# A token-mixing vision tower in one kernel: the last doubling of two tables cut in two, GpSimd's shift table started during the powers, new load orders

## What is computed

```python
# layer 1: a diagonal state-space kernel, 256 positions long, for each channel h
dA = (1 + dtA / 2) / (1 - dtA / 2)              # complex, (256, 64)
V = exp(log(dA)[:, :, None] * arange(256))      # powers 0 .. 255 of dA
h = 2.0 * einsum('chn,hnl->chl', C * B, V).real # (16, 256, 256)
# layer 2: attention without softmax (16 heads, elu + 1), MLP 256 -> 1024 -> 256, on layernorm(h)
h = h + attn_block(layernorm(h))
# layer 3: a soft decision tree of depth 8 (255 gates, 256 leaves), on layernorm(h)
h = h + tree_ffn(layernorm(h))
```

## Time and profile before

| what | before |
|---|---|
| median of 3 runs | 499.4 us (498.92 to 500.75) |
| profiled execution, its own time | 499.2 us |
| its span | 497.4 us |
| PE busy | 441.4 us, 89% |
| DVE busy | 347.8 us, 70% |
| ACT busy | 296.0 us, 60% |
| POOL busy | 191.1 us, 38% |
| DMA | 30.95 MB, 39903 packets |

### The profile page before, as it was taken

The page is one execution under the profiler, slowest core; times in us unless marked ns, Lnnn a source line. Parts: engine busy times, 40 slices in busy tenths (PEclk is TensorE's granted clock), DMA queues, the critical chain, the costliest instruction groups (busy, mean ns, idle before and its releaser), DMA issues.

```text
span 497.4 us, 11488 instructions
## 1 busy us (share of the span) xinstructions
PE 441.4 (89%) x3881; PEld 402.0 (81%) x3881; DVE 347.8 (70%) x814; ACT 296.0 (60%) x617; POOL 191.1 (38%) x188
## 2 busy tenths in 40 slices
PE   0375778999999999999999999999999999998985
PEld 0165667887798898989989988988988988988984
DVE  4899987987876786546486486476476476485775
ACT  4734655879867686358438348348347357356542
POOL 0299996742423011417207207207206306306120
PEclk9867999999999999999999999999999999999996
DMA  4532678436353102001002002002002001001002
GB/s 128 180 137 76 169 187 228 99 97 169 95 138 98 43 22 63 2 2 43 0 2 84 0 0 84 0 0 84 0 0 84 0 0 42 0 0 45 0 2 84
DMA packets 39903, 30.95 MB, mean 62 GB/s; under 512 B 19520, under 2 KB 35264, under 8 KB 39872
## 3 DMA queue, kind: packets, MB, share of 16 engines
q1 hardware_dynamic: 28944, 27.48, 18.6%
q10 hardware_dynamic: 10928, 3.08, 2.7%
HBM read 17.97 MB, written 12.58 MB: 61 GB/s over the span
## 4 chain that ended last, share of the span: by engine, by line
PE 69%; DVE 11%; issue 5%; POOL 5%; ACT 5%; DMA 3%; SPq 1%; POOLq 0%; DVEq 0%; ACTq 0%
PE PS L336 19%; PE PS L338 18%; PE PS L337 18%; PE PS L1655 5%; PE PS L1780 3%; PE PS L1697 3%; PE PS L1628 2%; POOL Wb L514 2%; DVE XY L1052 2%; DVE lTl L1348 1%; POOL Wa L514 1%; DMA aim<-in_a_im 1%; DMA craw<-in_c_ri 1%; PE PS L1664 1%; DVE PS L1052 1%
## 5 line engine op out<-in xcount | busy, mean ns | idle before, releaser
L1377 DVE TENSOR_TENSOR gl<-PS,gh 128x512 fp32r<-128x512 f32 x56 | 38.7, 690 | 62.3 <-ACT gh L867 31.9
L864 ACT ACTIVATE PS<-PS,fc1bias 128x512 f32<-128x512 f32 x56 | 36.7, 655 | 75.3 <-PE PS L338 74.4
L336 PE MATMUL PS<-fc2h,gh 128*128 128x256 f32 x256 | 73.6, 288 | 2.9 <-DVE gl L1377 1.5
L567 POOL TENSOR_SCALAR pst<-mv 128x4 f32<-128x4 f32 x15 | 4.2, 283 | 185.1 <-DVE pst L1361 185.1
L338 PE MATMUL PS<-fc2l,gh 128*128 128x256 f32 x256 | 71.5, 279 | 0.0
L337 PE MATMUL PS<-fc2h,gl 128*128 128x256 f32 x256 | 71.4, 279 | 0.0
L336 PE MATMUL PS<-x2Th,fc1h 128*128 (+2 forms) x144 | 54.5, 379 | 0.0
L336 PEld LDWEIGHTS PS<-fc2h,gh 128*128 128x128 f32 x256 | 48.0, 188 | 7.0 <-DVE pst L1361 1.6
L337 PE MATMUL PS<-x2Th,fc1l 128*128 (+2 forms) x144 | 53.0, 368 | 0.0
L338 PE MATMUL PS<-x2Tl,fc1h 128*128 (+2 forms) x144 | 52.9, 367 | 0.0
L337 PEld LDWEIGHTS PS<-fc2h,gl 128*128 128x128 f32 x256 | 48.2, 188 | 1.0
(11 more groups left out here) (256 smaller groups left out, 1408.9 us busy)
## 6 DMA issues: line engine op xcount, KB each, us to landing
h<-h_scratch SPq DMA_DIRECT2D x16, 256.0 KB, 3.4
q_scratch<-qe SPq DMA_DIRECT2D x16, 256.0 KB, 2.3
qf<-q_scratch SPq DMA_DIRECT2D x16, 256.0 KB, 2.9
out_tokens<-outb SPq DMA_DIRECT2D x14, 256.0 KB, 2.3
h_scratch<-tokev ACTq DMA_DIRECT2D x10, 256.0 KB, 3.1
craw<-in_c_ri SPq DMA_DIRECT2D x16, 128.0 KB, 2.5
craw<-in_c_ri SPq DMA_DIRECT2D x32, 64.0 KB, 2.4
h_scratch<-tokev SPq DMA_DIRECT2D x6, 256.0 KB, 2.9
```

What stands on the lines that cost most here:

```text
L336: pe.matmul(dst, ah, bh, start=start, stop=False, **kw)
L864: act.activation(bank(j % 2), bank(j % 2), ACT.Gelu, bias=fc1bias[:, j:j + 1]).then_inc(gact, 1)
L1377: dve.tensor_tensor(gl[:, j % 2, :], bank(j % 2), gh[:, j % 2, :].bitcast(F32), ALU.subtract).then_inc(gldone, 1)
```

## The change

It has five parts, and the diff below is cut to their core.

1. **X and Y.** The third doubling (m = 4) is done for channels 0 to 127 before chunk 0, and for channels 128 to 255 (chunks 8 to 15) behind the sum of chunk 7. ACT copies the powers for the second half into bank 6 in chunk 0, and waits for the second half before it puts out the tables of chunk 8. The first doubling uses bank 0 for its products, the third bank 2.
2. **The shift table.** POOL starts after the sixth instruction of the powers instead of after the last, forms the third power into a row of its own, reads the first three powers from the compact table, and no longer waits for ACT's copies. ACT makes eight copies into Er and Ei later, behind the copy for the third doubling. DVE waits for them before chunk 0.
3. **PSUM.** The imaginary parts of the powers 8, 16 and 32 and of U are kept in PSUM.
4. **Loads.** One half of the imaginary input goes over SP in front of the others, and two of the four loads of B over ACT; the qkv weights go behind B. Later, chunk 11's coefficients and chunk 12's go between the first loads of images, one after each of the first two.
5. **Orders behind chunk 9.** On ACT the tables of chunk 12 move ahead of the result of chunk 10, and the operands of chunk 12 behind the first `y_high`; on DVE statistics and low parts are interleaved with the products of chunks 11 and 12. PE does the second half of the bias matmuls only when the first product of chunk 0 is done.

```diff
@@ power(): where the powers lie
+        def u_imag(d):
+            return (PS[:, 2, H:2 * H], PS[:, 3, 0:H], PS[:, 3, H:2 * H])[d]
...
+                return [pwb[:, j - 3, 0, :], (PS[:, 6, H:2 * H], PS[:, 7, H:2 * H], PS[:, 2, 0:H])[j - 3]]
+            return [U[:, 0, j - 6, :], u_imag(j - 6)]
@@ sync
-            sp.dma_start(qkvraw[:, :, :], qkvT.rearrange("(k p) o -> p k o", p=P)).then_inc(ld_qkv, 16)
+            sp.dma_start(aim[halves[1], :], a_im).then_inc(ld_aim, 16)
             for r, rows in enumerate(halves):
                 sp.dma_start(btab[rows, 0, :], b_ri[r]).then_inc(ld_b, 16)
-                sp.dma_start(btab[rows, 1, :], b_ri[1 - r]).then_inc(ld_b, 16)
+            sp.dma_start(qkvraw[:, :, :], qkvT.rearrange("(k p) o -> p k o", p=P)).then_inc(ld_qkv, 16)
...
-            for n in range(2, FIRST):
+            for n in range(2, FIRST - 1):
                 load_c(n // 2, n % 2)
             for par in range(2):
                 sp.wait_ge(h0st[par], CREDIT + 16 * (PAIRS // 2))
-            for s in range(4):
+            for s in range(2):
                 load_h0(s)
-            load_c(FIRST // 2, FIRST % 2)
+                load_c((FIRST - 1 + s) // 2, (FIRST - 1 + s) % 2)
+            for s in range(2, 4):
+                load_h0(s)
@@ gpsimd
-            pool.wait_ge(dve_set, DVE_POWERS)
-            rotated(Er[:, :, 2], Ei[:, :, 2], pw[:, 0, 0, :], pw[:, 0, 1, :], pw[:, 1, 0, :], pw[:, 1, 1, :],
+            pool.wait_ge(dve_set, DVE_Z + 6)
+            rotated(pw[:, 2, 0, :], pw[:, 2, 1, :], pw[:, 0, 0, :], pw[:, 0, 1, :], pw[:, 1, 0, :], pw[:, 1, 1, :],
                     tE[:, :, 0])
-            pool.wait_ge(e_out, 6)
@@ scalar
+            act.dma_start(aim[0:N, :], a_im).then_inc(ld_aim, 16)
             for r in range(2):
-                act.dma_start(aim[r * N:(r + 1) * N, :], a_im).then_inc(ld_aim, 16)
+                act.dma_start(btab[r * N:(r + 1) * N, 1, :], b_ri[1 - r]).then_inc(ld_b, 16)
...
+            act.wait_ge(pool_set, 1 + 6)
+            for e in range(4):
+                for x, t in enumerate((Er, Ei)):
+                    w = pw4[:, x, :] if e == 3 else pw[:, e, x, :]
+                    act.activation(t[:, :, e], w, ACT.Copy).then_inc(e_out, 1)
             act.wait_ge(pe_set, 1)
...
             act.wait_ge(gated, 1)
+            act.activation(PS[:, 6, H:2 * H].rearrange("p (x h) -> p x h", x=2), pwb[:, 2, :, P:H],
+                           ACT.Copy).then_inc(pw_out, 1)
             opened(0, 1)
...
             closed(3, 0)
             paired_operands(4, 0)
+            closed(3, 1)
+            act.wait_ge(dve_set, DVE_XY)
+            for par in range(2):
+                paired_tables(4, par)
             m_unshifted(4, 0)
...
+            tables(SINGLE + 2)
             token_row(SINGLE)
-            tables(SINGLE + 2)
+            y_high(0)
             operands(SINGLE + 2)
-            y_high(0)
@@ vector
+            dve.wait_ge(pw_out, 3)
+            doubled(slice(0, P), 4, *(w[:, 0:P] for w in halves_of(1)), bank(2))
...
+            dve.wait_ge(e_out, 8)
...
-            for n in range(6, SINGLE - 1):
-                overlapped(n, n % 2)
+            overlapped(6, 0)
+            product_sums(7, 1)
+            dve.wait_ge(pw_out, 4)
+            doubled(slice(P, H), 4, PS[:, 6, H:H + P], PS[:, 6, H + P:2 * H], bank(2))
+            assert count[0] == DVE_XY, count[0]
+            dve.wait_ge(pool_set, POOL_TABLES + 6)
+            first_product(8, 0)
+            second_product(8, 0)
+            overlapped(8, 0)
             product_sums(SINGLE - 1, 1)
...
             unsummed_products(SINGLE)
+            norm1_stats(0)
             single_product(SINGLE + 1, 0)
             single_product(SINGLE + 1, 1)
-            norm1_stats(0)
+            norm1_apply(0)
             single_sums(SINGLE + 1)
-            norm1_apply(0)
+            single_product(FIRST, 0)
             norm1_stats(1)
+            y_low(0)
+            single_product(FIRST, 1)
             norm1_stats(2)
-            y_low(0)
             for n in range(FIRST, CHUNKS):
                 s = n - FIRST
-                single_product(n, 0)
-                single_product(n, 1)
+                if s > 0:
+                    single_product(n, 0)
+                    single_product(n, 1)
+                single_sums(n)
                 if s == 0:
                     norm1_apply(1)
                     norm1_apply(2)
-                single_sums(n)
@@ tensor, the bias matmuls
             for j in range(JH):
+                if j == JH // 2:
+                    pe.wait_ge(prodX, CREDIT + 1)
```

More of the change, by code:

```diff
@@ L52 @@
 DVE_U = DVE_POWERS + 4 + 4 + 4 + 5
-DVE_W1 = DVE_U + 3
+DVE_XY = DVE_U + 5
+DVE_W1 = DVE_XY + 3
 DVE_W2 = DVE_W1 + 2 + KD
@@ L178, in vit_tower @@
         pw = sb("pw", [P, 3, 2, H])
+        pw4 = sb("pw4", [P, 2, H])
         phase1_end = max(phase1_end, cursor[0])
@@ L318, in sums_before @@
             return max([x for x in range(c) if sums_bank(x) == sums_bank(c)], default=-1)
+        def u_imag(d):
+            return (PS[:, 2, H:2 * H], PS[:, 3, 0:H], PS[:, 3, H:2 * H])[d]
         def power(j):
-            if j < 3:
+            if j < 2:
                 return [pw[:, j, x, :] for x in range(2)]
+            if j == 2:
+                return [pw4[:, x, :] for x in range(2)]
             if j < 6:
-                return [pwb[:, j - 3, x, :] for x in range(2)]
-            return [U[:, 0, j - 6, :], ui[:, j - 6, :]]
+                return [pwb[:, j - 3, 0, :], (PS[:, 6, H:2 * H], PS[:, 7, H:2 * H], PS[:, 2, 0:H])[j - 3]]
+            return [U[:, 0, j - 6, :], u_imag(j - 6)]
         def apart(eng):
@@ L648, in _ @@
             act.activation(Y[:, :, 0], btab[:, 1, :], ACT.Copy, scale=-2.0).then_inc(b_out, 1)
+            act.wait_ge(ld_qkv, 16)
+            act.activation(qkvh[:, :, :], qkvraw[:, :, :], ACT.Copy).then_inc(act_set, 1)
             act.wait_ge(ld_const, 16 * 6)
             act.activation(minus[:, :], ident, ACT.Copy, scale=-1.0).then_inc(minus_set, 1)
-            act.wait_ge(ld_qkv, 16)
-            act.activation(qkvh[:, :, :], qkvraw[:, :, :], ACT.Copy).then_inc(act_set, 1)
             act.wait_ge(dve_set, DVE_Z)
@@ L666, in _ @@
             act.wait_ge(dve_set, DVE_POWERS)
-            for j in range(2):
-                act.activation(bank((6, 7)[j]), pwb[:, j, :, :].rearrange("p x h -> p (x h)"),
-                               ACT.Copy).then_inc(pw_out, 1)
-            for e, j in ((0, 0), (1, 1), (3, 2)):
-                for x, t in enumerate((Er, Ei)):
-                    act.activation(t[:, :, e], pw[:, j, x, :], ACT.Copy).then_inc(e_out, 1)
+            act.activation(PS[:, 6, 0:H], pwb[:, 0, 0, :], ACT.Copy).then_inc(pw_out, 1)
+            act.wait_ge(dve_set, DVE_POWERS + 4)
             for d in range(ND - 1):
-                if d == 2:
-                    act.wait_ge(dve_set, DVE_POWERS + 4)
-                act.activation(U[:, 1, d, :], ui[:, d, :], ACT.Copy, scale=sgn[:, 0:1]).then_inc(u_out, 1)
+                act.activation(U[:, 1, d, :], u_imag(d), ACT.Copy, scale=sgn[:, 0:1]).then_inc(u_out, 1)
+            act.activation(pwb[:, 2, 1, :], PS[:, 2, 0:H], ACT.Copy).then_inc(u_out, 1)
+            act.activation(PS[:, 7, 0:H], pwb[:, 1, 0, :], ACT.Copy).then_inc(pw_out, 1)
             for c in range(3):
@@ L797, in _ @@
             paired_tables(1, 0)
-            with act.Fori(0, 3) as it:
+            with act.Fori(0, 2) as it:
                 for par in range(2):
                     next_opened(it, par)
-            paired_tables(4, 1)
+            next_opened(2, 0)
+            paired_operands(3, 1)
+            closed(2, 1)
+            m_unshifted(3, 1)
             closed(3, 0)
             paired_operands(4, 0)
+            closed(3, 1)
+            act.wait_ge(dve_set, DVE_XY)
+            for par in range(2):
+                paired_tables(4, par)
             m_unshifted(4, 0)
-            closed(3, 1)
             paired_operands(4, 1)
@@ L1117, in _, with halves_of @@
                     tt(y_, y_, t, ALU.subtract)
+            def halves_of(b):
+                return (PS[:, b, x * H:(x + 1) * H] for x in range(2))
+            dve.wait_ge(pw_out, 1)
+            doubled(slice(0, H), 1, *halves_of(6), bank(0))
+            dve.wait_ge(pw_out, 2)
+            dve.wait_ge(u_out, 4)
+            doubled(slice(0, H), 2, *halves_of(7), PS[:, 2:4, :].rearrange("p b x -> p (b x)"))
+            dve.wait_ge(pw_out, 3)
+            doubled(slice(0, P), 4, *(w[:, 0:P] for w in halves_of(1)), bank(2))
             assert count[0] == DVE_U, count[0]
```

33 lines of the change are left out of this document (16 added, 17 removed).

## The result

The changed kernel takes 500.8 us, the median of 20 runs (497.9 to 503.4), beside 498.4 us for the kernel before on the same chip (20 runs, 496.5 to 500.8). The ratio is 1.0047 with a 95% interval of 1.0030 to 1.0065: slower by about 2.3 us.

A forecast was written before the change was run, and what follows sets the result against it. Bound: DVE to chunk 0, POOL (DVE as full) to chunk 12, then PE. -3.74 start, +4.14 +0.62 +0.22 doubling and waits, +1.2 clock, -0.4 behind: +2.05, so 501.4 us against 499.4; whole range 497.3 to 503.2.

The forecast's parts named there:

- The case: Forecast case, chance 0.48: doubling returns in full behind chunk 7, PE idles, clock halves; own range 500.2 to 502.7 us.
- the signs that were named: First product 34.6, doubling 4.1 us, PE gap over 6, clock 0.50, chunk 8 3.7 us, POOL waiting, chunk 12 about 90.
- Start and first half of the doubling: Before chunk 0: first product at 34.57 instead of 38.31, 3.74 us earlier, bounds 3.1 and 4.9.
- Chunk 0 at full clock: PE, chunk 0: starts at 38.05 and expected at full clock, 2.10 us; otherwise 3.72 us.
- POOL then runs level with DVE up to chunk 7 and nothing is lost at chunk 8.: Fallback if chunk 0 takes 3.72 us instead of 2.10: POOL keeps level with DVE, no loss at chunk 8.
- Sum of chunk 9: DVE's sum of chunk 9 at 68.96 instead of 67.70: 1.26 us later.
- The clock at chunk 8: PE idle 6.6 us before chunk 8, then half clock, 3.72 us; +1.2 net, POOL's chunk 10 2.45 us later.
- Behind chunk 9: From POOL's chunk 10 to chunk 12's matmuls: -0.4 us, chunk 12 at 90.15 instead of 88.10.
- The loads: Chunk 12's coefficient stall of 2.1 us goes, chunk 8 takes its place; load waiting in SP's queue costs nothing.
- The imaginary parts in PSUM: DVE's instructions stay at 0.42 us with either source, so costed at nothing.
- The rival in which POOL was the bound: Chance 0.12: second half of doubling lies in DVE's spare time, 5.5 us carry through, 493.9 us.
- The clock that stays up: Rival, chance 0.22 (shared with DVE's full start gain): PE keeps its clock over the hole, chunk 12 at 88.0, 499.3 us.

The follow-up runs named there:

- before_newstart: Kernel before with only the new order of first loads (imaginary input halved over two queues, two B loads on ACT, qkv weights behind): ratio 0.9956.
- tables_first: Changed kernel, but ACT puts out the tables of chunks 8 and 9 before taking out chunk 7's result: ratio 1.0024.
- bias_unsplit: Changed kernel without PE's wait for the first product in the middle of the bias matmuls: ratio 1.0042.
- warm_hole_full: Changed kernel with thirteen extra unused 256-column matmuls filling PE's hole before chunk 8: ratio 1.0022.
- full_unsplit: Changed kernel with the third doubling in one piece before chunk 0 and no wait inside the bias matmuls: ratio 0.9989.
- imag_in_sbuf: Changed kernel with the imaginary parts of powers 8, 16, 32 and of U back in SBUF: ratio 1.0054.
- full_unsplit_oldloads: full_unsplit with the old load order (chunk 11's coefficients ahead of the wait for stores, chunk 12's behind all four image loads): ratio 0.9968.
- tables_first_unsplit: Changed kernel, doubling still split, with the edits of tables_first and bias_unsplit together: ratio 1.0019.
- warm_hole: Changed kernel with nine extra unused 256-column matmuls in PE's hole between chunks 7 and 8: ratio 1.0064.
- mixedloads_filled: full_unsplit with chunk 11's coefficients before the store wait, chunk 12's behind the first image group, and four unused matmuls between the bias matmuls: ratio 0.9954.

## Why the prediction was right, and where it was not

The forecast was 501.4 us, 2.0 us more than the 499.4 us that it started from; measured are 500.8, and 2.3 us more than the kernel before beside it. The case was the likeliest one, by its mechanism: the doubling leaves the front, comes back in full behind chunk 7, and opens a hole on PE in which the clock falls. Of the signs that were named, the doubling of 4.1 us, the gap of over 6 us, the clock of 0.50 behind it and POOL's wait for PE are in the profile; the first product came earlier, and chunk 8 took 3.3 us and not 3.7. That the sum came so near is partly luck: a first product 1.33 us too early stands against 2.64 us more of waits up to the sum of chunk 9, and the clock took less than forecast. Its terms fared as follows.

- *Start and first half of the doubling.* 34.57 forecast, 33.24 in this profile and 33.26 to 34.56 in six others. The term of 3.74 us, with its bound of 4.9, was 5.07 here: fc1 landed 6.5 us after its issue and not 8.1, and PE began the products of weights at 25.74, so that ACT was free when DVE's doubling was done. The Trainium skill, "Trainium Kernel Development and Optimization", section Key Constraints, grants a second issuer the issue time alone. The prediction drew from it that 1.6 us of the start could be missing; before_newstart shows 2.2 us at chunk 0. The sentence itself is not contradicted. ACT issued both halves of the imaginary input before, the second at about 2.0 us, and it landed 6.3 us later, beside the 768 KB that SP had issued at 1.81. Now SP issues that half at 1.81, only 0.2 us earlier, the 768 KB at 3.71, and the halves land 3.0 and 3.6 us after their issue. So what fits the rows is that the large load now comes behind the small ones, more than the second issuer; the two were not tried apart.
- *Chunk 0 at full clock.* Wrong. The step said "as PE has just worked"; the clock fell during the one-column matmuls themselves (0.54 in the mean from 34 to 38 us), their second half took 3.57 us instead of 1.8, and chunk 0 started 0.7 us later than forecast and ran at 0.50.
- *"POOL then runs level with DVE up to chunk 7 and nothing is lost at chunk 8."* This is the step that failed. POOL began chunk 2 at 42.83, set the pace, and chunk 7's matmuls started behind it at 61.08, to end at 63.2. ACT, in order, takes their result out before it writes the tables of chunk 8, so DVE waited 2.34 us instead of 0.62. tables_first shows those 1.7 us. Where chunk 7's matmuls started earlier, the same wait was shorter: 1.95 us in bias_unsplit (60.85) and 1.52 in warm_hole_full (59.93). The fallback case was named, but followed to POOL only and not to the instruction behind POOL's on the next engine.
- *Sum of chunk 9.* +2.54 us instead of +1.26: -1.33 for the first product, +0.92 between it and sum 7 (24.33 us instead of 23.41; one wait of 0.60 for ACT's tables, at 45.34, is the larger part), and +1.72 for the tables of chunk 8. The doubling itself was 4.11 for 4.14.
- *The clock at chunk 8.* Forecast a hole of 6.6 us, half clock, 3.72 us and 1.2 us net. Measured 6.08, half clock at first and 3.30 us. The term is the lateness of POOL's chunk 10 less that of the sum of chunk 9, and by that measure it was 3.18 - 2.54 = 0.64 us, half of what was forecast. (The 1.2 us of warm_hole_full are another quantity: what the clock cost in all, for which the prediction had 1.85 us.) Chunk 8 started 1.31 us later than forecast, but its shorter time gave back 0.6 of it: POOL's chunk 10 at 72.76 instead of 72.03.
- *Behind chunk 9.* -0.4 us forecast; from POOL's chunk 10 (+3.18) to chunk 12 (+2.6) it was -0.6. Right.
- *The loads.* "This costs nothing" is right for the changed kernel, which has a hole in front of POOL's chunk 10, and wrong for the order itself: 0.8 us in full_unsplit, with POOL waiting for chunk 11's coefficients. The step looked at chunk 12 and the images and not at chunk 11, which had been moved behind the wait for the stores.
- *The imaginary parts in PSUM.* Nothing, as forecast (imag_in_sbuf).

The rival in which POOL was the bound fell: with 3 us of lead in POOL's stream the delay still came out whole. It has a grain of truth, for POOL paced chunks 2 to 7. The clock that stays up, built in warm_hole_full, gave chunk 12 at 88.33, where that rival had 88.0, but that agreement is chance, in a run whose chunk 0 was 1.1 us early.

So the change is slower for the split, and next for the wait in the bias matmuls, which would show without it. The start would have been a gain (0.4% faster alone). An earlier load of chunk 12, with chunk 11's left in its place, takes POOL's wait of 1.60 us away, but at chunk 12 it brings only 0.4 us, less than the scatter. The orders behind chunk 9 and the earlier shift table were not taken out one by one; full_unsplit_oldloads, which has both beside the new start, and before_newstart, which has neither, agree to 0.14 us at chunk 12, so together they are worth little. The scatter of the first product, 1.3 us between like kernels, goes with the end of the products of weights on PE, which ACT copies out ahead of the tables. In five of the seven it starts 1.30 or 1.31 us behind the first bias matmul, which stands right behind these products (34.56 behind 33.26 in tables_first); in the two earliest (33.24 and 33.26) DVE's own doubling ends at 32.6 us, as late as ACT's copy or later. How long the products take differs with the granted clock: tables_first_unsplit and warm_hole begin them at 26.40 and 26.41, the clock from 29 to 30 us is 0.84 and 0.50, and the bias starts at 31.38 and 32.87. Why the clock came back at such different times stays open.

## What to carry to other kernels

Work that is moved out of a start must land where its engine idles, and everything in order behind it on the engines that feed from it has to be followed one step further than the first wait: here the doubling cost 4.1 us as planned, and ACT's order and PE's clock took 2.9 us more. A part that tests as worth nothing may only be hidden by another (the bias wait: 0.2 us beside the split, not to be told from nothing, and 2.9 us without it), so undo suspects in pairs as well as one by one. And before a load is moved, look at what else now stands behind the wait in front of it.

## What the runs showed of the hardware that I had not expected

- The granted clock fell while PE was busy without a gap. In bias_unsplit, with one-column matmuls, it was 0.62 from 35 to 36 us and 0.50 from 36 to 37, with PE busy for 1.00 us in each; in mixedloads_filled it was 0.75 and 0.50. It is not so each time: the same 32 matmul records took 4.77 us in bias_unsplit and 3.63 in the kernel before.
- The clock fell after a pause of only 1.99 us in warm_hole, while in the changed kernel it was still at 1.00 some 4.8 us into the hole (67 to 68 us). In bias_unsplit, whose hole is as long (6.06 us), it was at 0.50 from 66 us on, 3 us into it. The time since the last matmul does not say alone when it falls.
- The end of the kernel has a clock of its own. In the profiled execution of the kernel before it fell there, in that of the changed kernel it did not. The same window of PE alone, first before, then after:

```profile
490.00:495.00 5.00, 4.01 (x18) 0.50 0.46 157
```

```profile
490.00:495.00 5.00, 3.45 (x28) 1.00 0.21 69
```

The two profiled spans differ by only 0.6 us (497.4 and 498.0) although chunk 12 is 2.6 us later. DVE's last addition into outb is still 2.06 us later than before (491.77 and 489.71), its last only 0.79 (495.00 and 494.21), so most of what was made up lies in these last microseconds. Two profiles set side by side would have called the change free, and the 20 runs of each did not.
